# DeepFM inference: gated weight loads, a tail in quarters, results turned by VectorE, and two fields of the last tile fetched row by row by SyncE

## What is computed

```python
lin = bias + x_num @ w_num + lin_cat[fid, x_cat].sum(axis=1)
vn = x_num[:, :, None] * v_num[None, :, :]
vc = v_cat[fid, x_cat]                      # 512 x 26 x 64: gathered rows
v = jnp.concatenate([vn, vc], axis=1)
sum_v = v.sum(axis=1)
interactions = 0.5 * (sum_v * sum_v - (v * v).sum(axis=1)).sum(axis=1, keepdims=True)
deep_in = jnp.concatenate([x_num, vc.reshape(vc.shape[0], -1)], axis=1)
h = jax.nn.relu(deep_in @ W1 + b1)          # 1677 -> 1024
h = jax.nn.relu(h @ W2 + b2)                # -> 512
h = jax.nn.relu(h @ W3 + b3)                # -> 256
deep_out = h @ Wo + bo
return lin + interactions + deep_out        # 512 x 1
```

## Time and profile before

| | us |
|---|---|
| median of 3 executions | 155.88 (154.91 to 156.05) |
| the profiled execution | 154.75 |
| its span, first to last instruction | 153.0 |

### The profile page before, as it was taken

How to read it: one execution, slowest core, us unless ns; L and a number is a source line. 1 busy time by engine, 2 the same in 40 slices (tenths; PEclk the granted TensorE clock), 3 DMA queues, 4 the chain that set the end, 5 groups by cost and what they waited for, 6 DMA issues and landing times.

```text
span 153.0 us, 2072 instructions
## 1 busy us (share of the span) xinstructions
PE 135.2 (88%) x661; PEld 105.0 (69%) x661; DVE 77.7 (51%) x216; ACT 58.0 (38%) x153; POOL 99.6 (65%) x111
## 2 busy tenths in 40 slices
PE   0303999879999999999999999999999999999994
PEld 0102776547776676888767878778787887776992
DVE  4310587997699687232435524333446223353712
ACT  4501578666376631142333132223431423234120
POOL 3777777777777777777777777777777777700000
PEclk9999999999999999999999999999999999999999
DMA  4999677987777643343234343431344433310000
GB/s 107 372 123 311 103 208 197 298 261 198 192 232 201 175 27 29 28 29 25 27 25 33 26 26 28 27 31 27 25 30 27 30 28 25 28 9 4 0 0 0
DMA packets 6750, 13.66 MB, mean 89 GB/s; under 512 B 2578, under 2 KB 2708, under 8 KB 6740
## 3 DMA queue, kind: packets, MB, share of 16 engines
q0 software_dynamic: 3328, 3.47, 25.6%
q1 hardware_dynamic: 3412, 10.07, 21.0%
HBM read 13.53 MB, written 0.00 MB: 88 GB/s over the span
## 4 chain that ended last, share of the span: by engine, by line
PE 67%; DVE 13%; DMA 12%; issue 3%; ACT 2%; POOL 1%; DVEq 0%
PE acc L593 12%; PE acc L590 12%; PE acc L583 11%; DMA raw<-in_weights 6%; DMA g<-in_table,rows 6%; DVE w_lo L371 4%; PE acc L659 4%; PE acc L655 3%; PE acc L656 3%; PE xt_ps L574 3%; PE acc L677 2%; DVE num_r L376 1%; ACT w_hi L234 1%; DVE hidden L412 1%; PE ht_ps L566 1%
## 5 line engine op out<-in xcount | busy, mean ns | idle before, releaser
L225 POOL DMA_INDIRECT g<-in_table,rows x104 | 98.8, 950 | 33.2 <-issue 28.3
L398 DVE TENSOR_TENSOR x_lo<-xt_ps,x_hi 128x128 fp32r<-128x128 f32 x52 | 15.0, 288 | 50.0 <-ACT x_hi L241 50.0
L241 ACT ACTIVATE x_hi<-xt_ps 128x128 fp32r<-128x128 f32 x52 | 14.3, 275 | 68.6 <-PE xt_ps L574 68.4
L590 PE MATMUL acc<-w_lo,x_hi 128*128 128x512 f32 x96 | 34.8, 443 | 0.0
L583 PE MATMUL acc<-w_hi,x_hi 128*128 128x512 f32 x96 | 31.1, 405 | 0.8 <-ACT x_hi L241 0.5
L593 PE MATMUL acc<-w_hi,x_lo 128*128 128x512 f32 x96 | 30.8, 402 | 1.0 <-DVE x_lo L398 1.0
L593 PEld LDWEIGHTS acc<-w_hi,x_lo 128*128 128x128 f32 x96 | 18.1, 191 | 6.0 <-DVE x_lo L398 1.8
L583 PEld LDWEIGHTS acc<-w_hi,x_hi 128*128 128x128 f32 x96 | 17.7, 191 | 5.4 <-ACT x_hi L241 1.4
L234 ACT ACTIVATE w_hi<-raw 128x1024 fp32r<-128x1024 f32 x18 | 19.0, 1055 | 6.2 <-DMA raw<-in_weights 6.1
L574 PE MATMUL xt_ps<-ident,g 128*128 128x128 f32 x52 | 14.4, 278 | 6.8 <-DMA g<-in_table,rows 6.8
L590 PEld LDWEIGHTS acc<-w_lo,x_hi 128*128 128x128 f32 x96 | 14.7, 193 | 4.9 <-issue 0.9
(11 more groups left out here) (99 smaller groups left out, 154.4 us busy)
## 6 DMA issues: line engine op xcount, KB each, us to landing
raw<-in_weights SPq DMA_DIRECT2D x18, 512.0 KB, 4.7
g<-in_table,rows POOLq DMA_INDIRECT x104, 3.4
hidden<-in_numeric SPq DMA_DIRECT2D x4, 108.1 KB, 7.0
consts<-in_row_consts SPq DMA_DIRECT2D x1, 129.0 KB, 9.2
cat<-in_x_cat SPq DMA_DIRECT2D x1, 39.0 KB, 4.3
cat<-in_x_cat SPq DMA_DIRECT2D x1, 13.0 KB, 1.7
out<-raw SPq DMA_DIRECT2D x1, 1.5 KB
out<-raw SPq DMA_DIRECT2D x1, 0.5 KB
```

The lines of the kernel that those rows point to most:

```text
L225: pool.indirect_dma_start(g[:, c, a * ROW:(a + 1) * ROW], None, table, bass.IndirectOffsetOnAxis(rows[:, t, 2 * c + a:2 * c + a + 1], 0))\
L241: act.activation(x_hi[:, n % SLOTS, :], xt(n), ACT.Copy).then_inc(xhi_done, 1)
L398: dve.tensor_tensor(x_lo[:, n % SLOTS, :], xt(n), x_hi[:, n % SLOTS, :].bitcast(F32), ALU.subtract).then_inc(xlo_done, 1)
L590: pe.matmul(acc[:, :], x_hi[:, n % SLOTS, :], w_lo[:, c, w], start=False, stop=False)
```

## The change

SP's loads are gated. Ahead of the first landed chunk only the indices of tile 0 and blocks 0 and 1 are issued; the other indices and block 2 follow when chunk 0 of tile 0 has landed, block 3 after chunk 1, blocks 4 and 5 after chunk 2, and the four copies of `numeric`, blocks 6 and 7 and the constants come after those. VectorE makes the row numbers of tile 0 before it zeroes `hidden`, and those of tiles 1 to 3 within tile 0. The work on the numeric columns moves back by one to three chunks.

Chunk 11 of tile 3 (two fields) is no longer gathered. The host hands over those 256 indices once more as one row; VectorE turns them into row numbers of the table in `late_row`, and SP loads them into registers, 32 at a time, and issues one DMA of 260 bytes for each, into a 14th place of `g`. `late_in` counts them; TensorE, ScalarE and VectorE wait for all 256 before they use that chunk.

In the tail layer 1's output goes in quarters of 256 columns instead of halves. The result is one add and one 32x32-block transposition by VectorE; `result_row` is gone from TensorE. The slots for `x_hi` and `x_lo` go from four to three.

```diff
-SLOTS = 4
+SLOTS = 3
+LATE = 2
+LATE_CHUNK = CHUNKS - 2
+LATE0 = 2 * LATE_CHUNK + 2 - LATE
...
         def chunk_landed(eng, t, c):
-            eng.wait_ge(rows_in[c], 32 * (t + 1))
+            if is_late(t, c):
+                eng.wait_ge(late_in, 16 * LATE * P)
+                if LATE == 1:
+                    eng.wait_ge(late_pool_in, 16)
+            else:
+                eng.wait_ge(rows_in[c], 32 * (t + 1))
...
+            chunk_landed(sp, 0, 0)
             sp.dma_start(cat[:, 1:TILES, :], by_tile[:, 1:TILES, :]).then_inc(cat_in[1], 16)
+            sp.dma_start(late_row[:, :], late_cat).then_inc(late_cat_in, 16)
             weight(2)
+            chunk_landed(sp, 0, 1)
+            weight(3)
+            chunk_landed(sp, 0, 2)
+            weight(4)
+            weight(5)
             sp.wait_ge(num_zeroed, 1)
-            for k in range(P // STACK):
-                sp.dma_start(hidden[k * STACK:k * STACK + NROWS, :], numeric).then_inc(num_in, 16)
-            weight(3)
+            numeric_stacks(0, 2)
+            weight(6)
+            numeric_stacks(2, 4)
+            weight(7)
             sp.dma_start(consts[:, :], row_consts).then_inc(consts_in, 16)
-            for i in range(RING, ITEMS):
+            numbers = [sp.alloc_register(f"late_number{i}") for i in range(STACK)]
+
+            def late_rows(first, end):
+                for n in range(first, min(end, LATE * P)):
+                    if n % STACK == 0:
+                        sp.load(numbers, late_row[0:1, n:n + STACK])
+                    a, p = 2 - LATE + n // P, n % P
+                    sp.dma_start(g[p:p + 1, CHUNKS, a * ROW:(a + 1) * ROW],
+                                 table[bass.ds(sp.snap(numbers[n % STACK]), 1), :]).then_inc(late_in, 16)
+
+            sp.wait_ge(late_ready, LATE)
+            for i in range(8, ITEMS):
                 weight(i)
+                late_rows(5 * (i - 8), 5 * (i - 7))
+            late_rows(5 * (ITEMS - 8), LATE * P)
...
+            for q in range(2):
+                act.activation(h1[:, quarter(q)], acc1[0][:, quarter(q)], ACT.Relu).then_inc(relu1a, 1)
+            for q in range(4):
+                act.wait_ge(h1t_done, 2 * LAST + q + 1)
+                act.activation(h1t_hi[:, 2 * q:2 * q + 2, :], quarter_ps[q][:, 0:QUARTER], ACT.Copy)\
+                   .then_inc(h1hi_done, 1)
...
+            def add_result(t):
+                dve.wait_ge(deep_done, t + 1)
+                dve.wait_ge(fm_done, t + 1)
+                dve.tensor_tensor(result[:, t:t + 1], deep[:, t:t + 1], fm[:, t:t + 1], ALU.add)\
+                   .then_inc(result_done, 1)
+
+            def turn_results(a):
+                dve.wait_ge(result_done, LAST + a)
+                dve.transpose(turned[:, a, :], result[:, :]).then_inc(result_turned, 1)
```

188 lines of the change are left out of this document (113 added, 75 removed).

## The result

The changed kernel takes **179.52 us** (median of four executions, 178.51 to 180.06); the kernel before took 155.45 beside it (154.91 to 156.05). The ratio is 1.157, with a 95% interval of 1.151 to 1.163. The prediction was 150.7, in a range of 148.8 to 155.5: wrong, and in the sign too. The ratios in this document leave out executions in a slower state (over 1.5% above the fastest of the same kernel), so a ratio can differ a little from that of two medians.

A forecast was written before the change was run, and what follows sets the result against it. TensorE's late start plus its own work was taken as the bound, with GpSimd's gathers 1.7 us behind. Gains of 3.9 (limited by gathers), 0.36 and 0.33 sum to 4.6 us, giving 150.7 us, range 148.8 to 155.5.

The forecast's parts named there:

- Part 4: SP's 256 row transfers for chunk 11 of tile 3: landed by 126.7 us, needed at 132.2, so hidden by 5.5.
- Part 1: Gated loads at the start: first turn at about 7.9 us, with 4.0 us gained by the end of tile 0.
- The cover: Slack of SP's row stream: 5.5 us, gone at 0.396 us per row, kernel slower than before from 0.418.
- the ring doesn't feel them: Rows between weight blocks 8 to 17: five rows and one block take 2.2 us, under a chunk's 2.5.
- From there tile 0 goes at the pace of gathers: Tile 0 after its gated first chunks: 2.5 us per chunk of two gathers, each landing in 4.6 us under weight traffic.
- the gate starves TensorE: Rival for tile 0: blocks 2 to 5 go out singly, its gain falls under 1.7 us, total about 152; chance 0.10.
- Part 2: Result by VectorE: three layer 1 steps each lose 0.74 us of TensorE work, 2.2 us in all.
- Part 3: GpSimd's gather stream with two gathers fewer: 102 gathers, the last issued at 130.1 us and landing at 133.4.
- the meeting point: Last tile's end: TensorE alone would gain 6.2 us, but the gathers limit the gain to 3.9 us.
- Part 5: The tail: quarters save 0.36 us before layer 2, the result by VectorE saves 0.33 us before the store.
- SyncE too slow: Rival for SP's rows: at 0.46 us a row the stream ends at 145.7, kernel takes 164 us; chance 0.20.
- TensorE loses pace while it waits: Rival for the last tile: idling for gathers slows matmuls for five steps and the tail, about 161 us; chance 0.04.

The follow-up runs named there:

- without SyncE's rows: The changed kernel with chunk 11 of tile 3 gathered by GpSimd again (104 gathers), gates, quarters and result by VectorE kept: 156.13 us, ratio 1.011 to the kernel before.
- the ungated start: The changed kernel with loads in the order of before and all 256 of SyncE's rows kept: 177.53 us, ratio 1.150 to the kernel before.
- the ungated kernel: The kernel before with quarters, result by VectorE and three x slots, loads in the old order, 104 gathers: 153.18 us, ratio 0.991.
- the kernel with the result alone: The kernel before with only the result added and turned by VectorE, TensorE's result matmuls gone: 153.76 us, ratio 0.995.

## Why the prediction was wrong, point by point

**Part 4, SyncE's rows: the step that failed.** The prediction summed 43.6 + 211 x 0.37 + 6 x 0.5 + 2.0 = 126.7 for the landing of the last row; it landed at 158.5, and what was to be hidden by 5.5 us was waited for 17.6 us. Term by term:

- *The start.* Block 17 was done at 55.0, not at 43.6: **11.4 us**. Of these, 4.0 are Part 1's gain, which did not come (below); 3.4 more the gated start loses by itself (done at 51.03 without SyncE's rows, 47.62 before); 4.0 lie between the gated kernels without and with the rows, 0.8 of them straight from the rows between the blocks. The first row stands another 0.2 behind the block.
- *A row.* 0.416 us instead of 0.37: 211 x 0.046 = **9.7 us**. The bound of the DMA itself was safe (0.225 measured, 0.30 taken); what surrounds it takes 0.19, not 0.07. I had priced one address instruction, and there are two, with three gaps. My 0.07 had no row behind it.
- *A register load.* The train takes 102.34; less 211 x 0.416 = 87.8 leaves 14.5 for six loads, 2.43 each with their surroundings instead of 0.5: **11.6 us**. I had kept 2.4 as the upper end and taken a value near the lower one, without a row for it. The floor of 0.6 us that the Trainium skill gives (DMA: Bandwidth & Descriptors, the section on the latency and other measured facts) holds as a floor only. The Trainium skill (Runtime: NRT & Kernel Launch, the section on instruction fetch mechanics) has about 0.2 us for every register of such a load, there from HBM, an estimate of 6.4 us for 32; these loads are from SBUF and took 2.12, or 0.066 a register.
- *The landing.* The last row is issued at 157.32 and lands 1.15 later, 0.9 behind the end of the train, instead of 2.0: 1.1 less.

Together 11.4 + 0.2 + 9.7 + 11.6 - 1.1 = 31.8, and 158.5 - 126.7 = 31.8. TensorE itself came to chunk 11 at 140.97 instead of 132.2, 8.8 later than forecast, since tile 0 lost where it was to gain; 8.8 + 17.6 of waiting + 2.65 of low clock are 29.1 of the 29.6 us by which the profiled execution (179.76) missed its 150.15. No single term would have been enough for this result. With the pace alone wrong the rows would have landed at 43.6 + 87.8 + 3 + 2 = 136.4, 4.2 late, and the kernel would have been about as fast as before. The cover that I had computed (gone at 0.396 us a row, slower from 0.418) was right as a formula; I had varied only one of its three terms in setting chances. And "the ring doesn't feel them" left no room for the two register loads among the 45 rows; from the ungated start it failed by some 5 us. The estimate from the Trainium skill's 512 cycles for a DMA instruction (DMA: Bandwidth & Descriptors, the section on why a DMA increments its semaphore by 16), 0.43 us, came near the pitch of 0.416 by luck: it is for the instruction alone, and that takes 0.225 here.

**Part 1, the gated loads.** The first turn at 8.14 was right (7.9 forecast), and so was chunk 1, whose matmuls start at 14.96 (13.8 to 15 forecast). The 4.0 us that were to be left at the end of tile 0 were not: the last turn of the tile came 5.9 us later than before, not sooner, 2.7 without SyncE's rows. The step that failed is "From there tile 0 goes at the pace of gathers": I took 4.6 us for a gather under weight traffic, from a stretch in which only weights were moved, and put no price on the numeric rows and the consts, which before had been loaded while TensorE had nothing to do anyway. After, gathers issued at 16 to 20 us take 10.2 on the median. Blocks come late as well: ScalarE waits for weight blocks 6.1 us in all in the kernel before, 7.5 in the ungated kernel, 16.3 gated without rows, 20.6 in the changed one (but 17.9 also in the ungated kernel with SyncE's rows between the blocks, so these waits tell that blocks are late and not why).

```profile
g<-in_table,rows POOLq DMA_INDIRECT x4, 10.2
```

This is the rival *the gate starves TensorE* (0.10), but its size was wrong as well: the gain of tile 0 was not under 1.7 us but negative. How much of the lag comes from TensorE's clock, which fell to 0.72 in 20 to 30 us, how much from the loads themselves, and how much from the numeric work that the change moved to later chunks, the runs don't separate. Only the first 1.8 us of lag, there at chunk 5 without SyncE's rows, come ahead of the moved work. So the cause of this part is argued from the landing times and not shown by a run of its own.

**Part 2, the result by VectorE.** Right: 3 x 0.74 = 2.2 us was forecast, and from 2.23 to 1.51 in each of three steps 2.2 were found.

**Part 3 and the meeting point.** Right in size: the last gather at 130.01 (130.1 forecast), and in the ungated kernel, with 104 gathers, the last turns wait for gathers by 0.67 and 0.87 us. In the changed kernel it never came to matter.

**Part 5, the tail.** The terms that the prediction names (1.6 + 0.24 + 0.42 + 0.39) make 2.65 and not 2.5, unless the high part overlaps the turns. Layer 2 starts 2.49 us after the last chunk's first matmul (137.60 to 140.09); 2.5 was forecast, 3.08 it was before and in the kernel with the result alone. The store's issue moved too, but not the end. From the last chunk's start to the issue of the store it was 12.77 before and is 12.24 in the ungated kernel, 0.53 of the 0.69 forecast. The kernel with the result alone has 12.50, so the result brings 0.27 (0.33 forecast) and the quarters 0.26 (0.36 forecast). From there to the end of the span 1.53 before and 1.96 now. The store of four rows of 32 takes 0.50 to issue where the store of one row took 0.26, and takes back 0.43 with its landing. I had not priced the store.

**The rivals.** *SyncE too slow* (0.20) came, beyond its 164 because two more terms were off; the row itself stayed under that rival's 0.46 us. *TensorE loses pace while it waits* (0.04) came on top of it, for the 17.6 us wait and not for the gathers of the last steps: the ungated kernel waits 0.67 and 0.87 us there and keeps its pace.

## What to carry to other kernels

Price an address taken from a register as the whole loop around the DMA, here 0.416 us a row and 2.4 for each load of 32 registers, and use a train of such rows only where it ends well ahead of its turn: 128 rows were hidden (61 us), 256 (124 us) were not, from either start. A gate that makes an early transfer faster may, as here, only move the crowd of the others; sum what it sets free, and look at what is on the path there, before counting its gain. Where a cover is thin, vary all of its terms together: three errors of 10 to 12 us each, all of one sign, met a margin of 5.5.

## What was not expected of the hardware

- A load of 32 registers on SP took 2.12 us (2.09 to 2.13), the DMA with an address from a register only 0.225, its neighbours 0.19 more.
- A 17.6 us wait cost 2.65 us more than itself: granted clock 0.50, and a step of 2.8 us for 1.5 behind it.
- With numeric rows, two weight blocks and consts under way together, gathers issued at 16 to 20 us took 10.2 us to land, the blocks 11.8 and the consts 12.2, against 4.6 for gathers beside weight blocks alone and 4.7 for the median block.
